# The first loads of x and W_e in fewer, longer transfers, and a later start for the sums of W_e on GpSimd, in a one-core matmul kernel

## Chip, cores and metric

The kernel runs on one core of a Trainium2 chip. The metric is the device time of one execution in microseconds (us), lower is better; the figure quoted is the median of several executions. The engines are named as in the profile: PE is TensorE, DVE is VectorE, ACT is ScalarE, POOL is GpSimd, and SP is the engine that issues all transfers here.

## What is computed

x has 128 x 128 x 512 floats (batch, position, feature), cond 128 x 512. The kernel adds to x a product with a weight matrix and a row that depends on cond:

```python
u = gelu(cond @ W_proj + b_proj)            # 128 x 512
W_u, W_e = weight_matrix[:512], weight_matrix[512:]
out = x + (u @ W_u)[:, None, :] + einsum('bnd,dc->bnc', x, W_e)
```

## The kernel before

**One position is one tile.** For a position n the 128 batch rows lie on the 128 partitions: x[:, n, :] is a tile of 128 x 512 floats. It is turned, so that features lie on partitions, and multiplied with W_e. The `x +` is folded in: `add_identity` adds the unit matrix to W_e (in the buffer `w_e`). Every product is made in three passes, because operands are split in a high part of a reduced format and the rest: high x high, high x low, low x high. Hence `w_hi` and `w_lo`, `x_hi` and `x_lo`.

**Head and quads.** The first 8 positions (four chunks of two) are multiplied plainly; the other 120 go in 30 quads of four positions by a Strassen-Winograd scheme with seven half-size products (`m1` to `m7`), which needs sums of quarters of W_e (`t_sum`, split into `t_hi` and `t_lo`) that GpSimd makes once, at the start.

**The start, which the change touches.** There is no scheduler: each engine has its list written out by hand and waits on semaphores.
- SP issues its transfers in the order of its list: two tiles of x (`direct`, L244 to L248), W_e in four (L249, one for each j; the row of partition p of W_e is 8 KB long, of which a j is 2 KB), two tiles of x more (L251), then cond, W_proj, b_proj, W_u, the rest of the head, and the first quads.
- PE runs six matmuls of zeros (`warm(WARM_UP)`, L653), turns the first two tiles of x into `direct_psum` (`flip`, L655 to L657), runs eight more matmuls of zeros (`warm(WARM_ON)`, L658), and then multiplies the first chunk (L663 to L684): for each j the two products with `x_hi` and the two with `x_lo` against `w_hi[j]`, and behind them the two with `w_lo[j - 1]`. Between stand the flips of the next two tiles of x (at j = 2) and of cond (at j = 3). Then come the product with W_proj (L690), the plain chunk 1 (L696 to L698) with the flip of h, the result of that product, in its middle (L706), the product with W_u (L712), chunks 2 and 3, and the quads.
- DVE adds the identity to part 0 of W_e, casts it to `w_hi[0]`, splits the two turned tiles of x (`split_direct`, L582), adds the identity to parts 1, 2 and 3 between and behind, and then makes the four `w_lo` (`split_w`, L587).
- ACT makes the high parts: `x_hi` of the direct tiles (L364), `w_hi` 1 to 3 (L370), `t_hi` (L377), and it copies h out of PSUM (L379), behind the `t_hi` in its list.
- POOL waits for the four identity additions (L312), makes the four `t_sum` (L313 to L318), then the four `t_lo` (L321), each behind its `t_hi`, and then the low parts of chunks 2 and 3 (L326).

Of the kernel before, what the change touches and what calls it, by code (L numbers as in the profile page):

```python
# [17 lines left out]
DIRECT = 2  # L18
# [4 lines left out]
def build_cond_residual(nc, x, cond, weight_matrix, w_proj, b_proj, out):  # L23
# [18 lines left out]
    NJ = D // P  # L42
# [15 lines left out]
    with ExitStack() as ctx:  # L58
# [82 lines left out]
        cond_loaded = sem("cond_loaded")  # L141
        w_proj_loaded = sem("w_proj_loaded")
        b_proj_loaded = sem("b_proj_loaded")
        w_e_loaded = [sem(f"w_e_loaded{j}") for j in range(NJ)]
        direct_loaded = [sem(f"direct_loaded{n}") for n in range(DIRECT * T)]
        direct_flipped = sem("direct_flipped")
        direct_hi_ready = sem("direct_hi_ready")
        w_u_loaded = sem("w_u_loaded")
# [83 lines left out]
        @block.sync  # L232
        def _(sp):
            def load_head(c):
                for q in range(NQ):
                    sp.dma_start(head_chunk(c)[Q * q:Q * (q + 1)],
                                 x_dram[q, :, :, c * T:(c + 1) * T, :]).then_inc(head_loaded[c], 16)

            def load_quad(k, p):
                for q in range(NQ):  # L240
                    sp.dma_start(raw_rows(quad_raw[p], QUAD)[Q * q:Q * (q + 1)],
                                 x_dram[q, :, :, bass.ds(HEAD + k * QUAD, QUAD), :]).then_inc(quad_loaded[p], 16)

            def load_direct(n):  # L244
                sp.dma_start(direct[:, n, :], x[:, n, :]).then_inc(direct_loaded[n], 16)

            for n in range(T):
                load_direct(n)  # L248
            for j in range(NJ):  # L249
                sp.dma_start(w_e[:, j, :], w_e_dram[:, j, :]).then_inc(w_e_loaded[j], 16)  # L250
            for n in range(T, DIRECT * T):  # L251
                load_direct(n)
            sp.dma_start(cond_sb[:, :], cond).then_inc(cond_loaded, 16)
            sp.dma_start(w_proj_sb[:, :, :], w_proj_dram).then_inc(w_proj_loaded, 16)
            sp.dma_start(b_proj_sb[:, :], b_proj_dram).then_inc(b_proj_loaded, 16)
            sp.dma_start(w_u[:, :, :], w_u_dram).then_inc(w_u_loaded, 16)
            load_head(2)
            load_head(3)
            load_quad(0, 0)
            load_quad(1, 1)  # L260

            sp.wait_ge(evacuated, 2)
            sp.dma_start(out[:, 0:QUAD, :], y[0][:, :, :]).then_inc(stored[0], 16)
            sp.wait_ge(a22_turned, 1)
            load_quad(2, 0)
            sp.wait_ge(evacuated, HEAD_CHUNKS)
            sp.dma_start(out[:, QUAD:2 * QUAD, :], y[1][:, :, :]).then_inc(stored[1], 16)

            def period(k, p, load, store):
                if load:  # L270

                    sp.wait_ge(a22_turned, k + 1)
                    load_quad(k + 2, p)
                if store:
                    sp.wait_ge(c12_out, k)
                    sp.wait_ge(c11_out, k)
                    sp.wait_ge(c21_out, k)
                    sp.dma_start(out[:, bass.ds(HEAD + (k - 1) * QUAD, QUAD), :],
                                 y[1 - p][:, :, :]).then_inc(stored[1 - p], 16)

            period(1, 1, True, True)
            with sp.Fori(1, QUADS // 2 - 1) as it:
                for p in range(2):
                    period(it * 2 + p, p, True, True)
            period(QUADS - 2, 0, False, True)
            period(QUADS - 1, 1, False, True)

            n = N - QUAD
            sp.wait_ge(c11_out, QUADS)
            sp.dma_start(out[:, n, left], y[1][:, 0, left]).then_inc(last_stored, 16)  # L290
            sp.wait_ge(c22_out, QUADS)
            sp.dma_start(out[:, n + T:n + QUAD, right], y[1][:, lower, right]).then_inc(last_stored, 16)
            sp.wait_ge(c12_out, QUADS)
            sp.dma_start(out[:, n:n + T, right], y[1][:, upper, right]).then_inc(last_stored, 16)
            sp.wait_ge(c21_out, QUADS)
            sp.dma_start(out[:, n + T:n + QUAD, left], y[1][:, lower, left]).then_inc(last_stored, 16)
            sp.wait_ge(c11_end_out, 1)
            sp.dma_start(out[:, n + 1, left], y[1][:, 1, left]).then_inc(last_stored, 16)
            sp.wait_ge(stored[0], 16 * (QUADS // 2 + 1))
            sp.wait_ge(stored[1], 16 * (QUADS // 2))  # L300
            sp.wait_ge(last_stored, 16 * 5)

        @block.gpsimd
        def _(pool):
            pool.memset(ident[:, :], 0.0).then_inc(ident_zeroed, 1)
            pool.wait_ge(ident_zeroed, 1)
            pool.affine_select(out=ident[:, :], in_=ident[:, :], compare_op=ALU.not_equal, fill=1.0,
                               base=0, pattern=[[-1, P]], channel_multiplier=1).then_inc(ident_ready, 1)

            b_of = w_e[:, :, :].rearrange("p (e j) (h c) -> p e h j c", e=2, h=2)  # L310
            b11, b12, b21, b22 = b_of[:, 0, 0], b_of[:, 0, 1], b_of[:, 1, 0], b_of[:, 1, 1]
            pool.wait_ge(w_diag_ready, NJ)  # L312
            pool.tensor_tensor(t_sum[0], b12, b11, ALU.subtract).then_inc(t_summed, 1)  # L313
            pool.tensor_tensor(t_sum[2], b22, b12, ALU.subtract).then_inc(t_summed, 1)
            pool.wait_ge(t_summed, 1)
            pool.tensor_tensor(t_sum[1], b22, t_sum[0], ALU.subtract).then_inc(t_summed, 1)
            pool.wait_ge(t_summed, 3)
            pool.tensor_tensor(t_sum[3], b21, t_sum[1], ALU.subtract).then_inc(t_summed, 1)  # L318
            for n in range(4):
                pool.wait_ge(t_hi_ready, n + 1)  # L320
                pool.tensor_tensor(t_lo[:, n, :, :], t_sum[n], t_hi[:, n, :, :].bitcast(F32),  # L321
                                   ALU.subtract).then_inc(t_lo_ready, 1)

            for c in range(2, HEAD_CHUNKS):
                pool.wait_ge(head_hi_ready, c - 1)
                pool.tensor_tensor(x_lo[c], x_t[c], x_hi[c].bitcast(F32), ALU.subtract).then_inc(head_lo_ready, 1)  # L326

            def prepare(k, p):
                pool.wait_ge(up_hi, k + 1)
                pool.tensor_tensor(slot(lo[p], UP, 2), a_up[p], slot(hi[p], UP, 2).bitcast(F32),  # L330
                                   ALU.subtract).then_inc(up_lo, 1)
                pool.wait_ge(s2_ready, k + 1)
                pool.tensor_tensor(s4[p], a12[p], s2[p], ALU.subtract).then_inc(s4_ready, 1)  # L333
                pool.wait_ge(s2_hi, k + 1)
                pool.tensor_tensor(slot(lo[p], S2), s2[p], slot(hi[p], S2).bitcast(F32),  # L335
                                   ALU.subtract).then_inc(s2_lo, 1)
                pool.wait_ge(s4_hi, k + 1)
                pool.tensor_tensor(slot(lo[p], S4), s4[p], slot(hi[p], S4).bitcast(F32),
                                   ALU.subtract).then_inc(s4_lo, 1)
                pool.wait_ge(s3_hi, k + 1)  # L340
                pool.tensor_tensor(slot(lo[p], S3), s3[p], slot(hi[p], S3).bitcast(F32),  # L341
                                   ALU.subtract).then_inc(s3_lo, 1)
                pool.wait_ge(a22_hi, k + 1)
                pool.tensor_tensor(slot(lo[p], A22), a22[p], slot(hi[p], A22).bitcast(F32),  # L344
                                   ALU.subtract).then_inc(a22_lo, 1)

            prepare(0, 0)
            prepare(1, 1)
            with pool.Fori(1, QUADS // 2) as it:
                for p in range(2):  # L350
                    prepare(it * 2 + p, p)
# [154 lines left out]
        def _(dve):  # L506
# [66 lines left out]
            dve.memset(zeros[:, :], 0.0).then_inc(zeros_ready, 1)  # L573

            def add_identity(j):
                dve.wait_ge(w_e_loaded[j], 16)
                diag = w_e[:, j, :].rearrange("p (a r) -> p a r", r=NJ)[:, :, j]
                dve.tensor_tensor(diag, diag, ident[:, :], ALU.add).then_inc(w_diag_ready, 1)

# [59 lines left out]
        def _(pe):  # L639
# [13 lines left out]
            warm(WARM_UP)  # L653
            pe.wait_ge(ident_ready, 1)
            for t in range(T):  # L655
                pe.wait_ge(direct_loaded[t], 16)
                flip(direct_psum[t], by_j(direct[:, t, :]), direct_flipped)  # L657
            warm(WARM_ON)  # L658

# [3 lines left out]
            for j in range(NJ + 1):  # L663
# [9 lines left out]
                        product(t, x_lo[0], w_hi, j)  # L673
                if j == NJ - 2:
                    for t in range(T):
                        pe.wait_ge(direct_loaded[T + t], 16)
                        flip(direct_psum[t], by_j(direct[:, T + t, :]), direct_flipped)
                if j == NJ - 1:
                    pe.wait_ge(cond_loaded, 16)
# [154 lines left out]
```

## Time and profile before

| | us |
|---|---|
| median of 3 runs | 348.48 (348.38 to 348.8) |
| the profiled execution | 347.61 |
| its span, first to last instruction | 345.8 |
| PE busy in it | 340.9 |
| POOL, DVE, ACT busy | 279.5, 260.6, 241.3 |
| data moved | 70.64 MB, mean 204 GB/s |

The profiled execution took 0.87 us less than the median of the three runs. The span is what the profile's times count from; 1.8 us of the execution lie outside it. A time such as 9.47 is counted in us from the start of the span. A matmul's end is modelled, so where several follow one another the starts say more than the durations.

### The profile page before, as it was taken

To read this page: it belongs to the slowest core of one execution; us is meant where nothing else is said; L and a number is where in the kernel's file an instruction comes from. 1 tells how busy PE (TensorE), PEld (TensorE's weight loads), DVE (VectorE), ACT (ScalarE), POOL (GpSimd) and SP (SyncE) were. 2 spreads that over 40 slices of the span, in tenths; PEclk is the share of its full clock that TensorE was granted. 3 is DMA by queue.
4 is the path that set the end of the run, shared out by engine and by line. 5 is a ranking of instruction groups with operands and counts; after the bars stand their busy time and mean duration, and the time that the engine had idled before them with its cause. 6 is when DMAs were issued, how large, how long until landed. Compare 5 with 4: busy or idle time off the path is not lost.

```text
span 345.8 us, 7739 instructions
## 1 busy us (share of the span) xinstructions
PE 340.9 (99%) x2670; PEld 328.6 (95%) x2670; DVE 260.6 (75%) x294; ACT 241.3 (70%) x413; POOL 279.5 (81%) x196
## 2 busy tenths in 40 slices
PE   8999999999999999999999999999999999999996
PEld 4676899999999999999999999999999999999996
DVE  2946997788777778877777887777788777778811
ACT  3451677877777787777778777777877777787741
POOL 0764899888989888898988889898888989888860
PEclk9999999999999999999999999999999999999999
DMA  7997769788898778789977888997787899778216
GB/s 215 353 218 166 172 184 251 203 209 201 174 243 223 211 200 215 193 171 243 224 211 200 214 196 168 243 224 208 205 212 197 167 243 225 210 204 210 83 55 227
DMA packets 72840, 70.64 MB, mean 204 GB/s; under 512 B 2944, under 2 KB 67456, under 8 KB 68608
## 3 DMA queue, kind: packets, MB, share of 16 engines
q1 hardware_dynamic: 72832, 70.53, 80.7%
q8 instruction: 5, 0.08, 0.1%
q14 instruction: 3, 0.02, 0.0%
HBM read 36.96 MB, written 33.55 MB: 204 GB/s over the span
## 4 chain that ended last, share of the span: by engine, by line
PE 85%; DVE 1%; issue 0%; ACT 0%
PE banks L728 29%; PE banks L730 28%; PE banks L732 28%; DVE work L508 0%; DVE banks L508 0%; DVE banks L550 0%; ACT snap_rows L462 0%; ACT y L503 0%; DVE y L519 0%; ACT hi L402 0%
## 5 line engine op out<-in xcount | busy, mean ns | idle before, releaser
L728 PE MATMUL banks<-t_hi,hi 128*128 128x256 f32 x480 | 136.1, 284 | 0.2 <-ACT snap_rows L462 0.2
L732 PE MATMUL banks<-t_hi,lo 128*128 128x256 f32 x480 | 136.0, 283 | 0.0
L730 PE MATMUL banks<-t_lo,hi 128*128 128x256 f32 x480 | 136.0, 283 | 0.0
L730 PE MATMUL banks<-w_lo,hi 128*128 128x256 f32 x360 | 102.0, 283 | 0.0
L732 PE MATMUL banks<-w_hi,lo 128*128 128x256 f32 x360 | 102.0, 283 | 0.0
L728 PE MATMUL banks<-w_hi,hi 128*128 128x256 f32 x360 | 102.0, 283 | 0.0
L508 DVE STREAM_TRANSPOSE work<-quad_raw 128x1024 f32<-128x1024 f32 (+1 forms) x60 | 97.3, 1621 | 0.0
L728 PEld LDWEIGHTS banks<-t_hi,hi 128*128 128x128 f32 x480 | 92.2, 192 | 0.6 <-issue 0.6
L730 PEld LDWEIGHTS banks<-t_lo,hi 128*128 128x128 f32 x480 | 92.2, 192 | 0.0
L732 PEld LDWEIGHTS banks<-t_hi,lo 128*128 128x128 f32 x480 | 92.2, 192 | 0.0
L330 POOL TENSOR_TENSOR lo<-work,hi 128x1024 fp32r<-128x1024 f32 x30 | 72.4, 2414 | 23.6 <-ACT hi L394 23.6
L402 ACT CAST hi<-work 128x512 fp32r<-128x512 f32 x120 | 68.7, 619 | 16.6 <-DVE work L558 8.6
L728 PEld LDWEIGHTS banks<-w_hi,hi 128*128 128x128 f32 x360 | 69.2, 192 | 0.0
L730 PEld LDWEIGHTS banks<-w_lo,hi 128*128 128x128 f32 x360 | 69.2, 192 | 0.0
L732 PEld LDWEIGHTS banks<-w_hi,lo 128*128 128x128 f32 x360 | 69.2, 192 | 0.0
L333 POOL TENSOR_TENSOR work<-work 128x512 f32<-128x512 f32 x30 | 39.0, 1298 | 18.8 <-DVE work L558 18.7
L445 ACT COPY banks<-banks 128x512 f32<-128x512 f32 x29 | 16.5, 570 | 43.9 <-PE banks L732 43.5
L566 DVE TENSOR_TENSOR y<-banks,snap_rows 128x512 f32<-128x512 f32 x30 | 20.7, 691 | 34.0 <-PE banks L732 34.0
L571 DVE TENSOR_TENSOR y<-banks,snap_rows 128x512 f32<-128x512 f32 x30 | 20.8, 692 | 27.7 <-PE banks L732 27.7
L341 POOL TENSOR_TENSOR lo<-work,hi 128x512 fp32r<-128x512 f32 x30 | 39.2, 1308 | 0.0
L344 POOL TENSOR_TENSOR lo<-work,hi 128x512 fp32r<-128x512 f32 x30 | 39.2, 1308 | 0.0
L335 POOL TENSOR_TENSOR lo<-work,hi 128x512 fp32r<-128x512 f32 x30 | 39.1, 1304 | 0.0
(74 smaller groups left out, 440.6 us busy)
## 6 DMA issues: line engine op xcount, KB each, us to landing
out<-y SPq DMA_DIRECT2D x31, 1024.0 KB, 4.8
quad_raw<-in_x SPq DMA_DIRECT2D x120, 256.0 KB, 5.8
head_raw<-in_x SPq DMA_DIRECT2D x4, 256.0 KB, 4.9
w_e<-in_L_cond_weight_matrix SPq DMA_DIRECT2D x4, 256.0 KB, 5.3
w_proj_sb<-in_L_cond_W_proj SPq DMA_DIRECT2D x1, 1024.0 KB, 9.1
w_u<-in_L_cond_weight_matrix SPq DMA_DIRECT2D x1, 1024.0 KB, 11.2
head_raw<-in_x SPq DMA_DIRECT2D x8, 128.0 KB, 9.1
out<-y SPq DMA_DIRECT2D x3, 256.0 KB, 2.2
```

The lines of the kernel that those rows point to most:

```text
L330: pool.tensor_tensor(slot(lo[p], UP, 2), a_up[p], slot(hi[p], UP, 2).bitcast(F32), ALU.subtract).then_inc(up_lo, 1)
L333: pool.tensor_tensor(s4[p], a12[p], s2[p], ALU.subtract).then_inc(s4_ready, 1)
L335: pool.tensor_tensor(slot(lo[p], S2), s2[p], slot(hi[p], S2).bitcast(F32), ALU.subtract).then_inc(s2_lo, 1)
L341: pool.tensor_tensor(slot(lo[p], S3), s3[p], slot(hi[p], S3).bitcast(F32), ALU.subtract).then_inc(s3_lo, 1)
L344: pool.tensor_tensor(slot(lo[p], A22), a22[p], slot(hi[p], A22).bitcast(F32), ALU.subtract).then_inc(a22_lo, 1)
L402: act.copy(slot(hi[p], at), source).then_inc(done, 1)
L508: return dve.transpose(out_, in_)
L566: dve.tensor_tensor(y[p][:, upper, right], c_bank[p], snap2[p][:, :, :], ALU.add).then_inc(c12_out, 1)
L571: dve.tensor_tensor(y[p][:, lower, right], a_bank[p], snap5[p][:, :, :], ALU.add).then_inc(c22_out, 1)
L728: pe.matmul(psum[:, t, :], a_hi[:, 2 * j + t, :], b_hi[:, j, :], start=False, stop=False, skip_group_check=True)
L730: pe.matmul(psum[:, t, :], a_hi[:, 2 * j + t, :], b_lo[:, j, :], start=False, stop=False, skip_group_check=True)
L732: last = pe.matmul(psum[:, t, :], a_lo[:, 2 * j + t, :], b_hi[:, j, :], start=False, stop=(j == T - 1), skip_group_check=True)
```

## The change

Three edits. The first four tiles of x come in two transfers of two tiles each (4 KB in a row for each partition, since two positions of a batch row lie side by side) in place of four, each with one semaphore. W_e comes in two transfers with two j each (also 4 KB a row) in place of four, each with one semaphore. And POOL, ahead of its first sum, waits for the last `w_lo` of DVE (L315 of the new text) in place of the four identity additions. No arithmetic changes.

```diff
-        w_e_loaded = [sem(f"w_e_loaded{j}") for j in range(NJ)]
-        direct_loaded = [sem(f"direct_loaded{n}") for n in range(DIRECT * T)]
+        w_e_loaded = [sem(f"w_e_loaded{n}") for n in range(2)]
+        direct_loaded = [sem(f"direct_loaded{c}") for c in range(DIRECT)]
...
-            def load_direct(n):
-                sp.dma_start(direct[:, n, :], x[:, n, :]).then_inc(direct_loaded[n], 16)
-
-            for n in range(T):
-                load_direct(n)
-            for j in range(NJ):
-                sp.dma_start(w_e[:, j, :], w_e_dram[:, j, :]).then_inc(w_e_loaded[j], 16)
-            for n in range(T, DIRECT * T):
-                load_direct(n)
+            def load_direct(c):
+                sp.dma_start(direct[:, c * T:(c + 1) * T, :],
+                             x[:, c * T:(c + 1) * T, :]).then_inc(direct_loaded[c], 16)
+
+            def load_w_e(n):
+                sp.dma_start(w_e[:, 2 * n:2 * n + 2, :], w_e_dram[:, 2 * n:2 * n + 2, :]).then_inc(w_e_loaded[n], 16)
+
+            load_direct(0)
+            for n in range(2):
+                load_w_e(n)
+            load_direct(1)
...
-            pool.wait_ge(w_diag_ready, NJ)
+
+            pool.wait_ge(w_lo_ready[NJ - 1], 1)
...
-                dve.wait_ge(w_e_loaded[j], 16)
+                dve.wait_ge(w_e_loaded[j // 2], 16)
...
-                pe.wait_ge(direct_loaded[t], 16)
+                pe.wait_ge(direct_loaded[0], 16)
...
-                        pe.wait_ge(direct_loaded[T + t], 16)
+                        pe.wait_ge(direct_loaded[1], 16)
```

The order of the instructions at two places. SP's queue at the start of the kernel, before (`head_raw` holds the tiles of x):

```order
1 L245 DMA head_raw<-in_x 128x512 x2
2 L250 DMA w_e<-in_L_cond_weight_matrix 128x512 x4
3 L245 DMA head_raw<-in_x 128x512 x2
4 L253 DMA cond_sb<-in_cond 128x512
5 L254 DMA w_proj_sb<-in_L_cond_W_proj 128x2048
```

and now:

```order
1 L245 DMA head_raw<-in_x 128x1024
2 L249 DMA w_e<-in_L_cond_weight_matrix 128x1024 x2
3 L245 DMA head_raw<-in_x 128x1024
4 L255 DMA cond_sb<-in_cond 128x512
5 L256 DMA w_proj_sb<-in_L_cond_W_proj 128x2048
```

Eight transfers ahead of that of cond have become four of twice the size, in the same order.

POOL's list from the identity matrix to the low parts of the head, before (`work` holds the `t_sum`):

```order
8 L307 AFFINE_SELECT ident<-ident 128x128
9 L313 TENSOR_TENSOR work<-w_e 128x512 [waits w_diag_ready]
10 L314 TENSOR_TENSOR work<-w_e 128x512
11 L316 TENSOR_TENSOR work<-w_e,work 128x512 [waits t_summed]
12 L318 TENSOR_TENSOR work<-w_e,work 128x512 [waits t_summed]
13 L321 TENSOR_TENSOR t_lo<-work,t_hi 128x512 [waits t_hi_ready] x4
```

and now:

```order
8 L309 AFFINE_SELECT ident<-ident 128x128
9 L316 TENSOR_TENSOR work<-w_e 128x512 [waits w_lo_ready3]
10 L317 TENSOR_TENSOR work<-w_e 128x512
11 L319 TENSOR_TENSOR work<-w_e,work 128x512 [waits t_summed]
12 L321 TENSOR_TENSOR work<-w_e,work 128x512 [waits t_summed]
13 L324 TENSOR_TENSOR t_lo<-work,t_hi 128x512 [waits t_hi_ready] x4
```

Nothing is moved on POOL; the first sum, and with it all that stands behind it, waits for another semaphore.

## Rows read from the trace of the kernel before

**Rows 1.** The page: PE's busy time, and the chain that ended last, by engine.
```profile
PE 340.9 (99%) x2670; PEld 328.6 (95%) x2670; DVE 260.6 (75%) x294; ACT 241.3 (70%) x413; POOL 279.5 (81%) x196
...
PE 85%; DVE 1%; issue 0%; ACT 0%
```

**Rows 2.** Waits of PE, 0 to 34 us and 34 to 346: in total, times, longest.
```profile
PE banks L661 <- DVE lo L582: 0.4, 1, 0.4
PE banks L661 <- DVE w_lo L587: 0.2, 1, 0.2
...
PE banks L728 <- ACT snap_rows L462: 0.2, 1, 0.2
```

**Rows 3.** Timeline of PE, 1.2 to 9.9 us: start, duration, then the instructions.
```profile
1.20 2.74 PE L642 MATMUL banks<-zeros 128*128 128x512 bf16 x6 [1.20 <-DVE zeros L573]
3.73 1.92 PE L646 MATMUL banks<-ident,head_raw 128*128 128x128 f32 x8
5.44 2.05 PE L642 MATMUL banks<-zeros 128*128 128x512 bf16 x8
7.46 0.73 PE L661 MATMUL banks<-w_hi,hi 128*128 128x512 f32 x2
...
9.28 0.63 PE L661 MATMUL banks<-w_hi,hi 128*128 128x512 f32 x2
```

**Rows 4.** Timeline of DVE, 6 to 9 us.
```profile
6.56 0.39 DVE L578 TENSOR_TENSOR w_e<-w_e,ident 128x128 f32<-128x128 f32 x1 [5.42 <-DMA w_e<-in_L_cond_weight_matrix]
...
8.21 0.68 DVE L582 TENSOR_TENSOR lo<-banks,hi 128x512 fp32r<-128x512 f32 x1
```

**Rows 5.** Timeline of SP's queue, 0 to 3.5 us.
```profile
0.74 0.87 SPq L245 DMA_DIRECT2D head_raw<-in_x  x2
1.65 1.86 SPq L250 DMA_DIRECT2D w_e<-in_L_cond_weight_matrix  x4
```

**Rows 6.** Issues of x tile 1, then W_e parts 0, 1, 3: us to landing.
```profile
head_raw<-in_x SPq DMA_DIRECT2D x1, 256.0 KB, 2.9
...
w_e<-in_L_cond_weight_matrix SPq DMA_DIRECT2D x1, 256.0 KB, 4.8
...
w_e<-in_L_cond_weight_matrix SPq DMA_DIRECT2D x1, 256.0 KB, 5.0
...
w_e<-in_L_cond_weight_matrix SPq DMA_DIRECT2D x1, 256.0 KB, 6.1
```

**Rows 7.** Stretches, all engines; last three columns: granted clock, DMA share, GB/s.
```profile
1.00:3.60 2.60, 2.40 (x6) 0.76 (x7) 0.14 (x1) 1.23 (x2) 0.29 (x1) 1.00 0.66 205
3.60:5.20 1.60, 1.60 (x8) 1.60 (x8) 0.00 (x0) 0.37 (x1) 0.00 (x0) 1.00 0.86 215
5.20:7.50 2.30, 2.30 (x12) 0.95 (x10) 0.91 (x3) 0.80 (x2) 0.00 (x0) 1.00 0.94 273
...
10.00:15.00 5.00, 5.00 (x28) 4.00 (x26) 5.00 (x4) 1.70 (x4) 4.92 (x4) 1.00 1.03 417
```

**Rows 8.** Timeline of DVE and POOL, 9 to 15.5 us: `split_w` 0 and 3, first sum.
```profile
9.47 0.70 DVE L587 TENSOR_TENSOR w_lo<-w_e,w_hi 128x512 fp32r<-128x512 f32 x1
...
13.48 1.77 DVE L587 TENSOR_TENSOR w_lo<-w_e,w_hi 128x512 fp32r<-128x512 f32 x1
...
9.66 1.66 POOL L313 TENSOR_TENSOR work<-w_e 128x512 f32<-128x512 f32 x1 [8.18 <-DVE w_e L578]
```

**Rows 9.** Timeline of PE, 14.4 to 19 us.
```profile
14.46 0.70 PE L661 MATMUL banks<-w_lo,hi 128*128 128x512 f32 x2
15.31 0.74 PE L661 MATMUL banks<-w_lo,hi 128*128 128x512 f32 x2 [0.15 <-DVE w_lo L587]
15.88 3.60 PE L690 MATMUL banks<-w_proj_sb,cond_t 128*128 128x512 f32 x8
```

**Rows 10.** Timeline of ACT, POOL and PE, 16 to 23 us: `t_hi`, `t_lo`, flip of h.
```profile
16.43 2.18 ACT L377 CAST t_hi<-work 128x512 fp32r<-128x512 f32 x4 [1.11 <-POOL work L318]
...
17.12 5.02 POOL L321 TENSOR_TENSOR t_lo<-work,t_hi 128x512 fp32r<-128x512 f32 x4 [0.73 <-ACT t_hi L377]
...
22.09 0.63 PE L646 MATMUL banks<-ident,snap_rows 128*128 128x128 f32 x4
```

## The prediction

> **What bounds the kernel now.** I read the page first: PE is busy 99% of the span, and the chain that ended last is PE for nearly all of its named share [rows 1]. So only what moves PE's work counts. Next the waits of PE: two short ones in the head, and one of 0.2 us in the first quads, behind ACT; none behind a transfer [rows 2]. Everything after the head is a row of matmuls that follow one another. A microsecond that the head gives or costs goes to the end unchanged, unless that wait in the first quads eats it. That wait hangs on DVE's work after the product with W_u, which moves with PE, so I let it move along.
>
> Then the start, in order of time. PE runs six matmuls of zeros, eight flips (two tiles, four each), eight matmuls of zeros, and starts the first real product at 7.46 [rows 3]. It does not wait for x at all in there. What it waits for is DVE: part 0 of W_e lands at 1.65 + 4.8 = 6.45 [rows 5, 6], DVE starts on it at 6.56 [rows 4], and a fixed sequence of short DVE operations ends with the second `split_direct` at 8.21 + 0.68 = 8.89 [rows 4], without which PE can't reach the products with j = 1, at 9.28 [rows 3]. **From 6.45 to 9.28 the path is landing of W_e, then DVE, 2.83 us.** From 9.28 PE is closely packed until the last `w_lo`: the pair with `w_lo[2]` starts at 14.46, that with `w_lo[3]` at 15.31, the W_proj product at 15.88 [rows 9].
>
> **The new wait of POOL.** In the trace `split_w` takes 0.70 when alone and 1.77 when POOL's sums run too; the last ends at 13.48 + 1.77 = 15.25 [rows 8]. With POOL held back all four should take the short time: 9.47 + 4 x 0.70 = 12.3 at the latest. The gain on PE is only what it waits for there. Two matmuls of 512 columns need some 0.57 from start to start of the next group (15.31 to 15.88), so unhindered the last pair would start at 14.46 + 0.57 = 15.03 in place of 15.31: **0.28 us saved**, the sum's first term. The row's own idle figure, 0.15 [rows 9], is the lower bound, and 0.3 the upper, since nothing else stands between these groups. The 3 us that DVE finishes earlier otherwise buy nothing.
>
> The price is on POOL. Its first sum moves from 9.66 [rows 8] to about 12.3. Its four sums then run alone, as `t_lo` does, at 5.02 / 4 = 1.26 each [rows 10]: done at 12.3 + 5.0 = 17.3. The `t_hi` of ACT follow, 2.18 [rows 10], to 19.6 against 18.6 before, and the copy of h stands behind them in ACT's list. A copy is about a quarter of the four `t_hi`, 0.55: h is ready at 20.2. PE wants it for the flip at 22.09 [rows 10]. That leaves 1.9 us of cover, 1.6 with PE 0.3 ahead. `t_lo` ends near 17.9 + 5.0 = 22.9 against 22.1; it is first needed by the quads, far behind. So I cost this at nothing, hidden by the first half of chunk 1 on PE; beyond 1.6 us more it would be PE's wait at the flip of h.
>
> **The x transfers.** PE's flips waited for tile 0 and then for tile 1, which lands at 1.17 + 2.9 = 4.1 [rows 5, 6]. Now both come with one semaphore. The bytes in front are the same and one issue of 0.43 is saved, so I take 4.0 (from 3.6, all bytes read, to 4.2). The flips start at 4.0 in place of 3.73, and the eight zeros behind them at 5.7 in place of 5.44; they end near 7.5 to 7.7 instead of 7.49 [rows 3]. DVE's low parts bound the third and fourth product anyway, so this costs nothing as long as the clock behaves (a rival, below). Tiles 2 and 3 are not waited for now [rows 2] and are issued 1.4 us earlier.
>
> **The W_e transfers.** This is the term that can't be read off. DVE now waits for parts 0 and 1 together, where it had part 0 at 6.45. Both ends come from rows. **Late end:** part 1 landed at 2.08 + 5.0 = 7.1 [rows 5, 6] with exactly the same bytes ahead of it (two tiles, parts 0 and 1, 1.05 MB in all). Nothing new stands in front, so 7.1, or +0.65. **Early end:** by 3.6 the queue had moved 2.6 x 205 = 0.53 MB, the two tiles. The W_e bytes behind them went at (1.6 x 215 + 2.3 x 273) / 3.9 = 249 GB/s in rows of 2 KB; the stretch with W_proj and W_u, in rows of 8 KB, went at 417 [rows 7]. At 249 the 1.05 MB are read at 5.8, and part 1 landed 1.3 later. At 417 the 0.52 MB would need 1.26 and land at 3.6 + 1.26 + 1.3 = 6.15, or -0.3; with a lag of 0.5, as tile 1 had, even 5.4. But PE's zeros end near 7.5, and four products need 0.9, so j = 1 can't start before 8.4: no more than -0.9. **Taken:** time per byte as a part for the row and a part for its length, 1/249 at 2 KB and 1/417 at 8 KB, gives 1/340 at 4 KB (an estimate from [rows 7]). 0.52 MB at 340 is 1.54, landing 6.4, or -0.05.
>
> The Trainium skill speaks against this gain: DMA: Bandwidth & Descriptors, Specifications, puts the least size for line rate at 512 B. By that rule 2 KB rows are as fast as 4 KB rows and the term would be +0.65, not -0.05. The rows at 249 against 417 don't agree with it, though the matrices and their places differ too.
>
> Parts 2 and 3 landed at 3.09 + 6.1 = 9.2 at the latest [rows 5, 6], just as DVE came to them; at 340 GB/s both are there 1.5 us after parts 0 and 1, near 8.0, and DVE wants part 2 at 8.8. No wait there. All later transfers are only issued earlier.
>
> **Sum.** -0.28 for `w_lo`, -0.05 for W_e, 0 for x, 0 for POOL: -0.33. Against the profiled execution's 347.61 that is 347.28. The runs' median is 0.87 above it, and I take the difference over: 348.48 - 0.33 = 348.15, said as **348.1**.
>
> **Rivals.**
> 1. W_e lands early. DMA goes at 417 with the short lag: -0.28 - 0.4 to -0.28 - 0.9, 347.3 to 347.8. For it: tile 1 lagged its bytes by only 0.5. Against: all W_e parts lagged by more than 1 us.
> 2. Longer rows bring nothing (the page's rule above): W_e at 7.1, +0.65 - 0.28 = +0.37, 348.85. For it: same bytes, same engines. Against: the two rates in [rows 7].
> 3. PE's clock rises later; this one ends slower. PE had no pause from 1.20 until the zeros ended. The first six zeros took 2.74 and the later eight 2.05, so about 0.43 against 0.22 apiece: 512 columns at 1.2 and then at 2.4 GHz, though the clock column says 1.00 all along [rows 3, 7]. Now a pause of up to 0.5 us opens ahead of the flips. If because of it the rise comes after the eight zeros, these take 8 x 0.43 = 3.4 and end at 5.7 + 3.4 = 9.1; the four first products at 1.2 GHz put j = 1 at 10.8 against 9.28: +1.5 - 0.28 = +1.2, 349.7. It decides once the rise slips past 6.7, where the zeros' delay exceeds what DVE hides. Against: a pause of 0.3 in 4 us is small. The Trainium skill (TensorE: Matmul & The Clock Gate, Part 1) says that the window in which activity is judged runs free of the kernel's start; by that the rise would vary by run rather than by this change, and the cost would be 0. One trace can't show it.
> 4. POOL slips further: the sums take 1.66 as before [rows 8], h comes 1.6 later, and uses up the cover: 0 to +0.3.
> 5. The change doesn't do what it says: `split_w` stays at 1.77 because something other than POOL slows it. Then 15.31 stays and POOL starts at 15.3, `t_hi` end near 22.5, h at 23.1, and PE waits 1 us at the flip: 349.4. Against: the one `split_w` that began before POOL took 0.70 [rows 8].
>
> **Chances.** About 0.2% of 348.5, or 0.7 us, is what a measurement of this kernel can tell from no change. The forecast (between -0.65 and +0.05) 0.45; rival 1 0.27, most of it beyond -0.7; rival 2 0.15; rival 3 0.08; rivals 4 and 5 0.05. With the edges of the forecast, faster 0.28, same 0.60, slower 0.12. The range runs from rival 1's end, 347.3, to rival 2's with 0.15 for the scatter of the runs, 349.0.
>
> **What the profile would show.** Right: four `split_w` of 0.70, done near 12.3; POOL's first sum right behind, its sums at 1.26; no wait of PE behind `w_lo`; first DVE operation on W_e at 6.5; SP through with its eighth old transfer 1.7 us sooner; the flip of h without a wait. Wrong: DVE's first operation on W_e after 7.0 or before 6.1; PE's second group of zeros longer than 2.4 us; a PE wait behind ACT's copy of h.

## The result, and the profile after

| | before | changed |
|---|---|---|
| median, us | 348.38 (7 runs, 348.02 to 348.80) | 347.20 (7 runs, 347.18 to 347.34) |
| ratio | | 0.9968, 95% interval 0.9958 to 0.9978 |
| the profiled execution | 347.61 | 347.27 |
| its span | 345.8 | 345.5 |

The change makes the kernel 1.2 us faster here (0.8 and 1.0 us in two repeats, below). The two traced executions differ by only 0.34 us. The prediction's 348.1 is too high, and its range ended 0.1 above the measured median. Two things stand out: the gain of the medians is more than three times that of the traces, and the scatter of the runs shrank from 0.8 to 0.16 us. Two executions far above all others (469.4 us of e2, and 666.1 us of the kernel before beside e16 and e17) are left out of the ranges and ratios below.

The trace of the changed kernel, timeline of PE, 3 to 19 us (start, duration, then the instructions):

```profile
4.41 1.95 PE L649 MATMUL banks<-ident,head_raw 128*128 128x128 f32 x8 [0.47 <-DMA head_raw<-in_x]
...
7.74 0.81 PE L664 MATMUL banks<-w_hi,hi 128*128 128x512 f32 x2
...
9.49 0.62 PE L664 MATMUL banks<-w_hi,hi 128*128 128x512 f32 x2
...
14.56 1.17 PE L664 MATMUL banks<-w_lo,hi 128*128 128x512 f32 x4
15.56 3.62 PE L693 MATMUL banks<-w_proj_sb,cond_t 128*128 128x512 f32 x8
```

DVE, POOL and ACT in the same stretch:

```profile
6.76 0.39 DVE L581 TENSOR_TENSOR w_e<-w_e,ident 128x128 f32<-128x128 f32 x1 [5.62 <-DMA w_e<-in_L_cond_weight_matrix]
...
9.59 2.49 DVE L590 TENSOR_TENSOR w_lo<-w_e,w_hi 128x512 fp32r<-128x512 f32 x4
...
12.16 1.28 POOL L316 TENSOR_TENSOR work<-w_e 128x512 f32<-128x512 f32 x1 [10.68 <-DVE w_lo L590]
...
19.40 0.58 ACT L382 COPY snap_rows<-banks 128x512 f32<-128x512 f32 x1
```

Its W_e transfers (KB, us from issue to landing; issued at 1.21 and 1.67), and two stretches (last column GB/s):

```profile
w_e<-in_L_cond_weight_matrix SPq DMA_DIRECT2D x1, 512.0 KB, 5.5
...
w_e<-in_L_cond_weight_matrix SPq DMA_DIRECT2D x1, 512.0 KB, 6.3
...
3.60:5.20 1.60, 1.13 (x5) 0.82 (x5) 0.00 (x0) 0.00 (x0) 0.00 (x0) 1.00 0.88 261
5.20:7.50 2.30, 2.30 (x13) 1.53 (x12) 0.70 (x2) 1.17 (x2) 0.00 (x0) 1.00 1.01 392
```

The W_proj product starts at 15.56 in place of 15.88 [rows 9], and that 0.32 is nearly the whole difference of the two traces. All four `w_lo` take 2.49 together where three of them had taken 1.8 each [rows 8]; PE no longer waits for the last. Against that W_e is touched 0.20 later than before [rows 4], and PE now pauses 0.47 ahead of the flips. The bytes go at 261 GB/s from 3.6 to 5.2 us and at 392 after it, in place of 215 and 273 [rows 7].

**One number reads a trace.** In all 20 traces of this study, of 12 different kernels, the execution's time minus the start of the W_proj product on PE is 331.68 to 331.80 us. The head decides every difference here, and all of it lies ahead of that product. Below, "W_proj at" is that start.

It can be split once more. Call the start of DVE's first operation on W_e the first touch. In seven traces with POOL late (changed, e1, e5, e7, e8, e9, e11) the W_proj product starts 8.76 to 8.81 after it; in four with POOL's old wait (before, e2, e13, e14) 9.21 to 9.32. So POOL's new wait is worth some 0.45 us in a trace, and the landing of W_e moves the rest one for one. The other traces have something else in between: a wait for part 3 or for a tile of x, zeros of PE that ended late, a clock that fell, or another order of DVE's list.

### The profile page after: what moved, and what is told of

Read it like the earlier page. It is cut to its first block, busy times and chain, and to the rows that moved or that the text cites. A ratio compares the mean times of both kernels' runs of the same rounds, so it can differ in the third digit from the quotient of the medians.

```text
span 345.5 us, 7735 instructions
## 1 busy us (share of the span) xinstructions
PE 340.3 (99%) x2670; PEld 328.6 (95%) x2670; DVE 257.4 (75%) x294; ACT 241.8 (70%) x413; POOL 278.1 (80%) x196
## 4 chain that ended last, share of the span: by engine, by line
PE 86%; DVE 1%; issue 0%; ACT 0%
PE banks L731 29%; PE banks L735 28%; PE banks L733 28%; DVE work L511 0%; DVE banks L511 0%; DVE banks L553 0%; ACT snap_rows L465 0%; ACT y L506 0%; DVE y L522 0%; ACT hi L405 0%
```

## The experiments

Each was run with executions of the kernel before beside it on the same chip.

| kernel | median (range), us | ratio to before, interval | traced: W_proj at, time |
|---|---|---|---|
| before, again (e0) | 348.17 (347.73 to 348.68) | 1.0002, 0.9993 to 1.0011 | 16.15, 347.91 |
| only POOL late (e1) | 347.92 (347.39 to 349.95) | 1.0002, 0.9990 to 1.0015 | 15.69, 347.39 |
| only the loads (e2) | 347.69 (347.27 to 348.14) | 0.9986, 0.9977 to 0.9996 | 15.87, 347.62 |
| changed, again (e5) | 347.35 (347.13 to 348.80) | 0.9984, 0.9972 to 0.9996 | 15.49, 347.23 |
| changed, x in four (e3) | 349.15 (348.02 to 351.06) | 1.0033, 1.0018 to 1.0047 | 19.30, 351.06 |
| changed, W_e in four (e4) | 347.75 (347.23 to 348.75) | 0.9993, 0.9981 to 1.0004 | 15.94, 347.73 |
| before, identity 3 later (e6) | 347.68 (347.23 to 348.47) | 0.9991, 0.9982 to 1.0000 | 15.78, 347.58 |
| e4 with identity 3 later (e7) | 346.96 (346.33 to 348.84) | 0.9976, 0.9958 to 0.9995 | 14.98, 346.76 |
| changed, identity 3 later (e8) | 347.32 (346.88 to 347.56) | 0.9971, 0.9959 to 0.9983 | 15.58, 347.31 |
| old loads, POOL late, identity 3 later (e9) | 348.01 (347.25 to 350.04) | 0.9999, 0.9983 to 1.0015 | 15.56, 347.36 |
| e7 again (e10) | 347.28 (346.58 to 348.63) | 0.9981, 0.9965 to 0.9997 | 14.80, 346.58 |
| changed, third time (e11) | 347.23 (347.10 to 347.43) | 0.9971, 0.9959 to 0.9982 | 15.50, 347.24 |
| changed, first x split first (e16) | 346.79 (346.47 to 347.05) | 0.9955, 0.9938 to 0.9971 | 15.04, 346.75 |
| e16 with six zeros (e17) | 346.78 (346.42 to 347.75) | 0.9953, 0.9938 to 0.9967 | 16.00, 347.75 |

### The two halves of the change, and the kernel before once more

e1 is the kernel before with the new wait, e2 the changed kernel with the old one:

```diff
-            pool.wait_ge(w_diag_ready, NJ)
+            pool.wait_ge(w_lo_ready[NJ - 1], 1)
```

> The old kernel with only the new wait of POOL. Theory A (the whole gain is the clash of DVE and POOL, and in most executions of the kernel before it costs more than the 0.3 us of the one trace): 347.2 to 347.4, 1.0 to 1.2 us under the kernel before, with a scatter as small as the changed kernel's 0.16 us. Theory B (the clash costs 0.3 us and the rest is the loads, which in most executions land later than in the one trace): 348.0 to 348.2, scatter as before, some 0.8 us. Both: four split_w of 0.7 us.

> The changed kernel with the old wait of POOL, so only the loads are changed. Theory A: 348.2 to 348.5, no gain, scatter of 0.8 us. Theory B: 347.4 to 347.6, scatter small, first DVE operation on W_e near 6.8 as in the changed kernel.

> The kernel before, unchanged, profiled a second time. Same as the kernel before within 0.05%. Of interest is its head: if its own time is near 348.4 and not 347.6, the two traces of the same program differ where the missing 0.8 us lies. Theory A: the first split_w beside POOL's first sum takes 1.8 us too, the last ends near 16.2 in place of 15.25. Theory B: DVE's first operation on W_e, 6.56, or its third identity addition, 9.2, comes up to 1 us later.

Timeline of DVE in e1, then of DVE and PE in e2:

```profile
9.71 2.50 DVE L587 TENSOR_TENSOR w_lo<-w_e,w_hi 128x512 fp32r<-128x512 f32 x4
```

```profile
9.46 5.78 DVE L590 TENSOR_TENSOR w_lo<-w_e,w_hi 128x512 fp32r<-128x512 f32 x4
...
15.29 0.73 PE L664 MATMUL banks<-w_lo,hi 128*128 128x512 f32 x2 [0.17 <-DVE w_lo L590]
```

The clash of DVE and POOL is where it was thought: with POOL late the four `split_w` take 2.5, without it 5.8, whatever the loads. But theory A falls: POOL's wait alone gives 0.2 us of median, inside its interval of no change, and leaves the scatter. That is less than the 0.45 that its wait is worth in a trace; the runs beside it, with a scatter over 1 us, don't show why. The loads alone give 0.4, clear of no change, and nine of ten executions within 0.52; the median 347.69 lies just above theory B's 347.4 to 347.6. The second trace of the kernel before names a first cause:

```profile
6.44 0.39 DVE L578 TENSOR_TENSOR w_e<-w_e,ident 128x128 f32<-128x128 f32 x1 [5.30 <-DMA w_e<-in_L_cond_weight_matrix]
...
9.45 0.39 DVE L578 TENSOR_TENSOR w_e<-w_e,ident 128x128 f32<-128x128 f32 x1 [0.38 <-DMA w_e<-in_L_cond_weight_matrix]
```

Part 3 of W_e came at 9.45, 0.25 later than in the first trace, and everything behind it on DVE, the low part 0 first, moved along.

### Which transfers must be long

e3 takes only x back to single tiles, e4 only W_e:

```diff
-            load_direct(0)
+            for n in range(T):
+                load_direct(n)
```

```diff
-            for n in range(2):
-                load_w_e(n)
+            for j in range(NJ):
+                sp.dma_start(w_e[:, j, :], w_e_dram[:, j, :]).then_inc(w_e_loaded[j], 16)
```

> The changed kernel, unchanged, a second time. Theory C (its gain of 1.15 us over the kernel before is whole and repeatable): 0.9 to 1.4 us under the kernel before, scatter under 0.4 us. Theory D (the parts add up: 0.1 us measured for the late POOL plus 0.4 for the loads): 0.5 to 0.8 us under.

> The changed kernel with the first tiles of x in four transfers again, so POOL late and only W_e in two. Theory E (the steadier and earlier landing of W_e's third and fourth part is what the loads give): within 0.2 us of the changed kernel, parts 2 and 3 landed before 8.7, scatter small. Theory F (it takes the tiles of x in 4 KB rows too, since they are ahead of W_e in the queue): 0.4 us or more over the changed kernel, DVE's first operation on W_e at 6.9 or later.

> The changed kernel with W_e in four transfers again, so POOL late and only x in two. Theory E: no better than the late POOL alone, 347.9 on that chip or 0.1 to 0.3 us under the kernel before, scatter of 0.8 us, part 3 of W_e landing near 9.2 or later. Theory F: within 0.2 us of the changed kernel.

The changed kernel gains 0.83 in e5, between theory C's 0.9 to 1.4 and theory D's 0.5 to 0.8 (0.97 in e11, below, is in C's). Seven of the nine executions of e5 lie between 347.13 and 347.51, two at 348.24 and 348.80; neither of the two was traced, and their cause is open. In e3, timelines of DVE and PE, and a stretch (granted clock, DMA share, GB/s last):

```profile
8.97 0.38 DVE L582 TENSOR_TENSOR w_e<-w_e,ident 128x128 f32<-128x128 f32 x1 [7.83 <-DMA w_e<-in_L_cond_weight_matrix]
...
9.87 0.73 PE L665 MATMUL banks<-w_hi,hi 128*128 128x512 f32 x2 [2.63 <-DVE w_hi L597]
...
12.20 1.05 PE L665 MATMUL banks<-w_hi,lo 128*128 128x512 f32 x2
...
3.60:5.20 1.60, 1.60 (x8) 1.60 (x8) 0.00 (x0) 0.37 (x1) 0.00 (x0) 1.00 0.64 155
```

Theory F is right about e3, and more sharply than it was put. W_e in long rows behind x in short rows is the worst of the four combinations: it lands at 8.9, PE pauses 2.6 us, and 2 us later runs for a while with 0.43 us a matmul (two in 0.85). The traced execution is the slowest of the twelve, 1.9 above their median, so W_e must land earlier in most. Theory F is wrong about e4, which it put within 0.2 us of the changed kernel: e4 is 0.4 slower than e5 beside it. With x long and W_e short part 0 lands at 5.9 and part 3 at 9.7, and DVE waits 1.04 us for it. So both loads have to be long.

### DVE's wait for part 3

In e6, e7, e8 and e9 one call is moved:

```diff
-            add_identity(3)
-            for j in range(NJ):
-                split_w(j)
+            split_w(0)
+            split_w(1)
+            add_identity(3)
+            split_w(2)
+            split_w(3)
```

> The kernel before, loads and POOL's wait as they were, with one thing moved: DVE adds the identity to part 3 of W_e behind split_w 0 and 1 instead of ahead of them. Theory G (in most executions of the kernel before, part 3 of W_e lands after 9.2 and holds up the low part 0, and through it PE): 0.2 to 0.5 us under the kernel before, no DVE wait for part 3. Theory H (part 3's landing costs nothing, part 0's does): no change, within 0.1 us.

> x in two transfers, W_e in four, POOL late, and the identity on part 3 moved behind split_w 0 and 1. Part 0 of W_e landed at 5.9 with these loads and part 3 at 9.7. Theory G: 1.3 to 1.8 us under the kernel before and 0.4 to 0.7 under the changed kernel, the W_proj product near 15.0. Theory H: as without the move, 0.3 to 0.5 us under the kernel before.

> The changed kernel with the same move. Both theories: no change against the changed kernel, within 0.15 us, since parts 2 and 3 have landed before DVE comes to them.

> The loads of the kernel before, but POOL late and the identity on part 3 behind split_w 0 and 1. Theory G in full (all that the new loads give is that PE no longer hangs on part 3 of W_e): as fast as the changed kernel run beside it, within 0.2 us, 0.8 to 1.1 us under the kernel before. Theory I (the loads give something else besides): 0.4 us or more over the changed kernel.

> x in two, W_e in four, POOL late, the identity on part 3 later, a second time, beside the changed kernel. If part 0's earlier landing is worth its 0.6 us: 346.7 to 347.0 and 0.3 us or more under the changed kernel. If the executions near 348.6 are a third of all again, the mean gain over the changed kernel vanishes.

> The changed kernel a third time, as the yardstick for the two others on the same chip: 0.8 to 1.2 us under the kernel before, all but a few executions within 0.4 us.

Timeline of DVE in e6, and its transfer of part 3, issued at 3.1:

```profile
8.85 1.29 DVE L587 TENSOR_TENSOR w_lo<-w_e,w_hi 128x512 fp32r<-128x512 f32 x2
10.11 0.39 DVE L578 TENSOR_TENSOR w_e<-w_e,ident 128x128 f32<-128x128 f32 x1
...
w_e<-in_L_cond_weight_matrix SPq DMA_DIRECT2D x1, 256.0 KB, 7.0
```

Part 3 landed at 10.1 and nobody waited. The move gives the kernel before 0.4 us of median (the interval reaches 1.0000) and the changed one nothing that shows (its ratio in e8 is that of e11): theory G, as far as one comparison goes. It is not the whole, and e9 doesn't repeat it: e9 has the old loads with POOL's wait and this one both taken care of, and is no faster than before, with executions from 347.25 to 350.04. e11 on the same chip is 0.78 faster, with all twelve within 0.33, and differs from e9 only in the loads and in this move, which costs the changed kernel nothing. So the loads give something besides (theory I). How much of it is what part stays open, since the scatter of the old loads is over a microsecond: by the medians, e1 and e2 give 0.2 and 0.4, and the whole change 0.8 to 1.2. e7 and e10 have the fastest executions up to here (346.33 and 346.58), since part 0 lands at 5.8 to 6.1, but a third of them lie at 348.2 or more. e7's median is 0.36 under e8's, e10's 0.05 over e11's, and by the ratios neither is ahead of the changed kernel; theory G's 1.3 to 1.8 us under the kernel before for e7 came out as 1.1. The late third was not traced.

### Traces of late executions

All traces of the old loads so far were of executions below 348. So four single executions were traced, three of the kernel before (e12 to e14) and one of e9's kernel (e15):

> The kernel before, one more trace. Theory J (in the executions near 348.4 part 0 of W_e lands after 6.9): in a trace above 348.1 DVE's first operation on W_e stands at 7.0 or later, and the time rises by what it is late. Theory K (it is part 3 alone): first operation at 6.3 to 6.9 and the fourth identity addition at 9.6 or later.

> The kernel before once more. Theory J: above 348.1, DVE's first operation on W_e at 7.0 or later. Theory K: first operation at 6.3 to 6.9, fourth identity addition at 9.6 or later.

> The kernel before once more. Theory J: above 348.1, DVE's first operation on W_e at 7.0 or later. Theory K: first operation at 6.3 to 6.9, fourth identity addition at 9.6 or later.

> Old loads with POOL late and the identity on part 3 later, one more trace. Here part 3 can't hold up low part 0. Theory J: time = 347.36 plus what DVE's first operation on W_e is later than 6.80. Theory K: 347.3 to 347.5.

They took 349.34, 348.81, 347.89 and (e15) 349.70. e13, transfers of x tile 1 and of part 0, timelines of DVE and PE:

```profile
head_raw<-in_x SPq DMA_DIRECT2D x1, 256.0 KB, 4.0
...
w_e<-in_L_cond_weight_matrix SPq DMA_DIRECT2D x1, 256.0 KB, 6.2
...
7.92 0.38 DVE L578 TENSOR_TENSOR w_e<-w_e,ident 128x128 f32<-128x128 f32 x1 [6.77 <-DMA w_e<-in_L_cond_weight_matrix]
...
17.13 2.31 PE L690 MATMUL banks<-w_proj_sb,cond_t 128*128 128x512 f32 x5
```

The same program as before, and part 0 is touched at 7.92 instead of 6.56: 1.36 later, and the execution is 1.20 longer. x was late too: tile 1 landed at 5.2 in place of 4.1. In e14 part 0 is touched at 6.93, 0.37 later, and the execution is 0.28 longer. Theory J describes these two. e12, timelines of DVE and PE, and a stretch in the middle:

```profile
5.90 0.39 DVE L578 TENSOR_TENSOR w_e<-w_e,ident 128x128 f32<-128x128 f32 x1 [4.76 <-DMA w_e<-in_L_cond_weight_matrix]
...
9.79 0.39 DVE L578 TENSOR_TENSOR w_e<-w_e,ident 128x128 f32<-128x128 f32 x1 [0.22 <-DMA w_e<-in_L_cond_weight_matrix]
...
10.83 1.06 PE L661 MATMUL banks<-w_lo,hi 128*128 128x512 f32 x2 [1.09 <-DVE w_lo L587]
...
10.80:13.40 2.60, 2.57 (x7) 1.88 (x7) 2.60 (x2) 0.04 (x1) 2.60 (x2) 0.55 1.03 423
```

Here part 0 is early, but parts 2 and 3 are late (DVE waits 0.93 and 0.22), PE pauses 1.09, and the clock column falls to 0.55 in the stretch behind. The late parts put the pair with `w_lo[0]` 0.60 behind that of the first trace (10.83 against 10.23); the W_proj product is 1.70 behind, and the other 1.1 is the clock. Late parts are theory K's mechanism, though its condition of a first touch at 6.3 to 6.9 isn't met. In e15 part 0 comes at 7.64, PE pauses 1.7 before its first product, and matmuls at 0.43 follow from 10.9 to 13.9; that lifts it to 349.70 where theory J alone gave 348.2. A mean granted clock of 0.995, as in e12 and e15, is rare: 4 of the 125 executions of the kernel before that ran beside the experiments have it, all above 349.7. So it isn't what the median loses.

What the median loses was not traced itself. 82 of those 125 took 348.00 to 348.74, and the five traces of the kernel before are of 347.61, 347.91, 347.89, 348.81 and 349.34 us. That the bulk has W_e or its later parts 0.4 to 1.1 us late is inferred from the traces on both sides.

### Two kernels that use what was found

With the landing steady, what stands between it and PE is DVE's list. e16 is the changed kernel with DVE's first x split moved into the time in which it waits for W_e; e17 has `WARM_ON = 6` besides:

```diff
             dve.wait_ge(ident_ready, 1)
+            split_direct(0)
             add_identity(0)
...
-            split_direct(0)
             add_identity(1)
```

> The changed kernel with DVE's low part of the first x tile ahead of the identity on part 0 of W_e: its input is ready at 6.1, W_e lands at 6.7, so it fills an idle stretch and takes 0.6 us off the path between W_e's landing and PE's products with j = 1. If that path is the bound: the W_proj product at 15.0 in place of 15.5, 346.8 us, 1.3 to 1.6 us under the kernel before, scatter as small as the changed kernel's. If PE's zeros (end near 7.7) bind instead: 347.0 to 347.2.

> As the one before, with six matmuls of zeros in place of eight after the flips. If the zeros bind: 0.1 to 0.3 us better than the one before. If PE's pause that opens instead costs the clock, some executions 1 to 2 us longer with a mean granted clock of 0.995.

e16, timelines of DVE and PE:

```profile
6.24 0.69 DVE L585 TENSOR_TENSOR lo<-banks,hi 128x512 fp32r<-128x512 f32 x1 [5.10 <-ACT hi L367]
6.85 0.38 DVE L581 TENSOR_TENSOR w_e<-w_e,ident 128x128 f32<-128x128 f32 x1
...
15.04 2.33 PE L693 MATMUL banks<-w_proj_sb,cond_t 128*128 128x512 f32 x5
```

346.79 us, 1.5 under the kernel before beside it, as expected where DVE's path is the bound. Its slowest execution, 347.05, is under the fastest of the changed kernel in any of its three comparisons, 347.10, and its W_proj product starts some 0.5 earlier. The two did not run on the same chip, though, and the intervals of their ratios overlap in part. Two zeros fewer add nothing to the median. The traced execution of e17 took 347.75, and PE shows why:

```profile
6.36 2.77 PE L645 MATMUL banks<-zeros 128*128 128x512 bf16 x6
```

Six zeros took 2.77, so 0.43 from one to the next, the 1.2 GHz level, though the mean granted clock of that execution is 1.000. The first products started at 8.56 in place of 7.75. The other eight executions took 346.42 to 346.82, so they did not lose this. The two missing zeros aren't the cause: the six that ran were slow already. The full clock simply came later here, which the mean granted clock doesn't show.

## Why the prediction was wrong

**The sum was right for the trace, and the trace was not the median.** The prediction's 347.28 for the profiled execution was measured as 347.27. The step that failed is the one that says "The runs' median is 0.87 above it, and I take the difference over". That 0.87 us was no fixed distance: the changed kernel's traced execution lies 0.07 above its median. So a change of -0.33 was forecast for the median, and -1.18 was measured (-0.83 and -0.97 in the repeats). The runs show in its place that the distance was time which the head of the kernel before lost in most executions, and which the new loads took away in large part: alone they give 0.4 us (e2), and with POOL and part 3 taken care of they are 0.78 ahead of the old ones and free of their scatter (e11 against e9). Where traced executions were late (e12 to e15), W_e or its later parts landed later than in the first trace; for the median one that is inferred. A warning stood in the times: the profiled execution was 0.77 faster than the fastest of the three runs, so the trace lacked something that the runs had. And a part of the 0.87 was the sample, since the five later groups of the kernel before have medians of 348.1 to 348.3.

The right sum for the trace was partly luck: `w_lo` gained more and W_e cost more than put, and the two errors nearly cancelled.

**W_e, taken as -0.05.** In the traces it is +0.20 (first touch 6.76 against 6.56), within the ends given. The landing at 6.4 assumed 340 GB/s from 3.6 us on; the stretch to 5.2 went at 261. What was left out is its scatter. In the nine traces with both loads in 2 KB rows (before, e0, e1, e6, e9, e12 to e15) the first touch lies between 5.90 and 7.92; in the five with all in 4 KB rows and DVE waiting for them (changed, e2, e5, e8, e11) between 6.64 and 6.81. The middle one of the nine is 6.80, hardly later than the steady 6.7; what differs is the late side (three of the nine at 6.93 or more) and the late parts behind an early one (e0, e12).

**"Parts 2 and 3 ... No wait there."** True of the changed kernel (landed at 1.67 + 6.3 = 8.0, as put). For the kernel before, the prediction saw that part 3 landed at 9.2 "just as DVE came to them" and gave it no price, though no slack in one trace can be a wait in another: DVE waited 0.38 for it in e0, 0.22 in e12. e6 shows 0.4 us for it, which e9 doesn't repeat.

**`w_lo`, -0.28.** From the pair with `w_lo[2]` to the W_proj product it was 15.88 - 14.46 = 1.42 and is 15.56 - 14.56 = 1.00: -0.42, beyond the upper bound of 0.3. The 0.57 that was taken for a pair of matmuls came from one behind a wait; packed, a pair takes 0.50. With the +0.20 of W_e and 0.1 gained between, the trace's -0.32 comes out.

**x, 0.** Tiles landed at 0.75 + 3.5 = 4.25, not 4.0; PE paused 0.47, and DVE's chain hid it, as said.

**POOL, 0.** Its sums ended at 17.28 (put at 17.3), the copy of h began at 19.40 and ended at 20.0 (put at 20.2), and no wait of PE for it appeared.

**Rival 2** took its rule on 512 B from the Trainium skill (DMA: Bandwidth & Descriptors, Specifications). It did not come true: W_e landed at 6.7 and not 7.1, and with all loads in 4 KB rows the stretch 5.2 to 7.5 went at 376 to 392 GB/s (five traces) against 248 to 321 in 2 KB rows (nine). But it isn't a transfer's own rows alone: in e3, with W_e in 4 KB rows behind x in 2 KB rows, the same stretch went at 240. **Rival 1** came nearest to the measured 347.2 with its early end, 347.3, by the wrong road: in the changed kernel W_e landed at 1.21 + 5.5 = 6.7, no earlier than part 0 before. **Rival 3**, a late full clock, is real: e17 lost 1 us to it. In the changed kernel's traces the eight zeros took 1.89 to 2.25 and nothing was lost, since DVE's chain hid it. A clock that fell later, which the prediction did not have, showed in e3, e12 and e15. **Rivals 4 and 5** did not occur.

## What to carry to other kernels

Hold the profiled execution's time against the runs before reading its stalls: where it lies below their range, the trace may lack a stall that the median has, and a second and third trace of the same program are worth more than a finer reading of the first. Where a transfer lands just as its consumer comes to it, count on a wait in some executions. In a head where the rest of the kernel is one packed row of matmuls, find the one instruction whose start fixes the end, and compare that.

## What the runs showed of the hardware

- Row length ahead in the queue matters to what is behind. By traces, first touch of W_e: x 2 KB and W_e 2 KB, 5.90 to 7.92; x 2 KB and W_e 4 KB, 8.97 (one trace, but all twelve executions of e3 took 348.0 or more); x 4 KB and W_e 2 KB, 5.86 to 6.17 (three traces) with part 3 at 9.67 in e4; both 4 KB, 6.64 to 6.81 (five). Why short rows of x delay long rows of W_e was not settled: the profile gives no landing for each of the 16 DMA engines.
- The clock fell to the 1.2 GHz level, 0.43 us a matmul of 512 columns, after a pause of PE: in e12 right behind one of 1.09 us, in e15 and e3 some 2 us after the end of one of 1.7 and 2.6. It rose again some 3 us later. A pause of 1.14 in e14 was not followed by it, nor were the shorter ones of the changed kernel and e13.
- At the start the first six zeros stand 0.43 apart in all traces though the clock column says 1.00. The full clock then came at different times in different executions: in e17 all six later zeros were still 0.43 apart, up to 8.5 us.
- DVE operations with two SBUF operands and POOL's slowed each other: 1.77 in place of 0.70 for the one [rows 8] and 1.61 to 1.74 in place of 1.28 for the other. Those of DVE with a PSUM operand did not: two took 1.28 beside POOL (e0, at 15.45) and 1.29 without it (the changed kernel). The Trainium skill (SBUF — State Buffer, SBUF: two separate sides) calls the ports that the two share an exclusive lock, held for a whole instruction, when DVE has two SBUF inputs; the traces agree for those with two SBUF inputs, and the ones with a PSUM operand weren't held up.
